# Scale-table quotients moved beside the attention outputs, and the maxima over partitions moved to TensorE, in a transformer layer kernel

## The reference

```python
x = hidden_states                       # (2, 1024, 1024) f32
xn = layernorm(x)
def bitnet_linear(x, weight, scale):    # q, k, v, o
    s = maximum(mean(abs(weight), axis=1), 1e-8)
    y = einsum('bsi,oi->bso', x, sign(weight / s[:, None])) * (s * scale)
    return nan_to_num(y, nan=0.0, posinf=1e6, neginf=-1e6)
# attention: 32 query heads, 8 key/value heads, head size 32, softmax(q k^T / sqrt(32)) v, then o
# feed forward: gate_w, up_w (1024, 3584), down_w (3584, 1024), int 0..15,
# zero point and scale for each group of 128 rows
def dequantize(w, scales, zeros):
    return (w - repeat(zeros, 128, axis=0)) * repeat(scales, 128, axis=0)
ffn = (silu(xn @ gate) * (xn @ up)) @ down
out = x + attention(xn) + ffn
```

## Time and profile before

| | |
|---|---|
| median of 3 runs | 2414.04 us (2412.61 to 2415.01) |
| the profiled execution's own time | 2414.68 us |
| its span, first to last instruction | 2412.7 us |
| PE busy | 2345.1 us (97%) |
| DVE busy | 1812.9 us (75%) |
| ACT busy | 1586.6 us (66%) |
| POOL busy | 963.6 us (40%) |
| mean granted TensorE clock | 0.994 |
| chain that ended last, by engine | PE 91%, DVE 4%, ACT 3%, issue 2% |

### The profile page before, as it was taken

How to read it: one execution, slowest core, us unless ns; L and a number is a source line. 1 busy time by engine, 2 the same in 40 slices (tenths; PEclk the granted TensorE clock), 3 DMA queues, 4 the chain that set the end, 5 groups by cost and what they waited for, 6 DMA issues and landing times.

```text
span 2412.7 us, 32718 instructions
## 1 busy us (share of the span) xinstructions
PE 2345.1 (97%) x12408; PEld 954.4 (40%) x12408; DVE 1812.9 (75%) x2313; ACT 1586.6 (66%) x2050; POOL 963.6 (40%) x533
## 2 busy tenths in 40 slices
PE   6999999999999999988999999999999999999998
PEld 3444233333333333323444444444444444444444
DVE  7878777777777777776467777777777777777777
ACT  5774777777777777774256666666665666666664
POOL 0000689999999999973012222220001222222000
PEclk9999999999999999999999999999999999999999
DMA  5220455555565555544311111131113211115111
GB/s 180 73 62 1 96 84 90 82 90 84 82 88 87 88 85 87 88 68 114 111 48 35 35 48 40 35 114 35 35 61 123 70 35 36 35 35 191 37 35 70
DMA packets 179857, 174.73 MB, mean 72 GB/s; under 512 B 87586, under 2 KB 127394, under 8 KB 179702
## 3 DMA queue, kind: packets, MB, share of 16 engines
q1 hardware_dynamic: 117430, 150.62, 20.3%
q0 software_dynamic: 62272, 22.03, 11.6%
HBM read 160.08 MB, written 65.45 MB: 93 GB/s over the span
## 4 chain that ended last, share of the span: by engine, by line
PE 91%; DVE 4%; ACT 3%; issue 2%; DMA 0%; SPq 0%; DVEq 0%; ACTq 0%; POOLq 0%
PE ps L1559 32%; PE ps L1575 16%; PE ps L1416 10%; PE ps L1361 10%; PE ps L1405 9%; PE ps L1429 5%; PE ps L1529 4%; PE ps L1381 3%; ACT zone L708 1%; DVE zone L973 0%; ACT zone L756 0%; ACT zone L822 0%; PE ps L1591 0%; DVE zone L1064 0%; ACT xT L678 0%
## 5 line engine op out<-in xcount | busy, mean ns | idle before, releaser
L1559 PE MATMUL ps<-xT,zone 128*128 128x512 f16 x3584 | 774.6, 379 | 2.7 <-DVE zone L1304 2.7
L1086 DVE TENSOR_REDUCE zone<-ps 128x1 f32<-128x512 f32 x1024 | 639.4, 683 | 178.7 <-PE ps L1361 178.6
L822 ACT ACTIVATE zone<-ps,sm 128x512 f32<-128x512 f32 x1024 | 626.8, 691 | 193.5 <-PE ps L1405 180.5
L599 POOL TENSOR_TENSOR zone<-zone 128x1024 f32<-128x1024 f32 x252 | 621.4, 2568 | 183.7 <-ACT zone L822 103.1
L1281 DVE TENSOR_SCALAR ps<-ps,zone_c 128x1024 f32<-128x1024 f32 x392 | 506.7, 1293 | 160.7 <-PE ps L1559 158.6
L889 ACT ACTIVATE ps<-ps,zone_c 128x1024 f32<-128x1024 f32 x392 | 426.7, 1088 | 259.9 <-PE ps L1559 259.9
L1559 PEld LDWEIGHTS ps<-xT,zone 128*128 128x128 f16 x3584 | 350.3, 98 | 426.2 <-DVE zone L1304 4.2
L1405 PE MATMUL ps<-zone 98*128 98x512 f16 x1024 | 388.3, 382 | 18.7 <-ACT zone L822 17.6
L1361 PE MATMUL ps<-zone 96*128 96x512 f16 x1024 | 388.3, 383 | 0.5 <-DVE zone L1086 0.4
L1575 PE MATMUL ps<-zone 128*128 128x512 f16 x1792 | 387.1, 379 | 0.0
L1292 DVE TENSOR_SCALAR ps<-ps,zone_c 128x1024 f32<-128x1024 f32 x216 | 279.3, 1293 | 93.0 <-PE ps L1575 92.8
(11 more groups left out here) (134 smaller groups left out, 1267.1 us busy)
## 6 DMA issues: line engine op xcount, KB each, us to landing
zone<-dequantised SPq DMA_DIRECT2D x84, 512.0 KB, 3.7
dequantised<-zero_points SPq DMA_DIRECT2D x84, 256.0 KB, 4.1
zone<-zone SPq DMA_DIRECT2D x384, 32.0 KB, 2.3
zone<-_attn_hidden_states_dram SPq DMA_DIRECT2D x16, 512.0 KB, 7.6
zone<-inverse_sums SPq DMA_DIRECT2D x128, 64.0 KB, 2.1
attention<-zone SPq DMA_DIRECT2D x32, 256.0 KB, 2.0
xT<-attention SPq DMA_DIRECT2D x4, 2048.0 KB, 11.9
dequantised<-in_L_ffn_gate_w_dram POOLq DMA_DIRECT2D x28, 256.0 KB, 6.2
```

Of the source, the lines that this page charges most:

```text
L599: nc.gpsimd.tensor_tensor(duo[n % 3], prob[:, prob_slot(e), :], prob[:, prob_slot(e + 2), :], add).then_inc(s["sum_ok"], 1)
L822: A(prob[:, prob_slot(e), m % 2 * 512:(m % 2 + 1) * 512], ps[:, 3 + m % 3, :], ACT.Exp, scale=gam[:, 0:1]).then_inc(s["exp_ok"], 1)
L1086: V.tensor_reduce(mxs[:, u % 2, half, i % 16:i % 16 + 1], ps[:, (2 * i + half) % 3, :], AX, amax).then_inc(s["max_ok"], 1)
L1559: last = MM(ps[:, 4 * s2 + 2 * m + c, :], ring[:, buf, m * H + g * P:m * H + (g + 1) * P], xT[:, hf, part, g, c * 512:(c + 1) * 512], star ...
```

## The change

- VectorE's `table_quotients` is cut into eight parts, `quotients(0)` to `quotients(7)`, which run behind the guards of outputs 13, 15, ... 27. `tab_ok` comes at the end of part 7. Nothing waits for it any more but ScalarE, after the last output.
- The maxima over partitions leave GpSimd. TensorE transposes the 128x56 maxima (`turn_maxima`, unit 30, behind step 11), VectorE reduces them along the row and scales a diagonal with them (`common_maxima`, its step 10), TensorE multiplies the diagonal with ones in four matmuls (`spread_maxima`, behind step 14), and VectorE multiplies the two halves (`common_product`, its step 11). Output 1 waits for that, as it uses the same PSUM bank.
- `load_wo(1)` follows `load_wo(0)` at step 15 of unit 30.
- The third round of `pair_sums` of unit 31 goes between the matmuls of output 0, the fourth behind output 1. ScalarE evacuates the sums behind output 1 and makes `head_of(30)` behind output 0; SP's three DMAs of the last inverse sums move from before output 0, 1 and 2 to 1, 2 and 4; VectorE's `invert(31)` moves from behind output 1 to behind output 2.

```diff
# SP
-                if u == UNITS - 1 and k == 3:
-                    sp.wait_ge(s["tab_ok"], 1)
                     load_wo(1)
...
-            compact_sums(UNITS - 1)
             for n in range(OUTPUTS):
                 if n == 1:
+                    compact_sums(UNITS - 1)
+                elif n == 2:
                     store_inverse(UNITS - 1)
-                elif n == 2:
+                elif n == 4:
                     spread_inverse(UNITS - 1)
# GpSimd
-            def common_maxima():
-                pool.wait_ge(s["pmx_ok"], 1)
-                nc.gpsimd.partition_all_reduce(pmr, pmx, P, RMAX).then_inc(s["pmr_ok"], 1)
-                pool.wait_ge(s["pmx_ok"], 2)
-                nc.gpsimd.partition_all_reduce(pmr2, pmx2, P, RMAX).then_inc(s["pmr_ok"], 1)
...
-                    if u == UNITS - 2 and j == 3:
-                        common_maxima()
# ScalarE, behind evac_attention(n)
                 if n == 0:
+                    head_of(UNITS - 2)
+                elif n == 1:
                     evacuate_sums(UNITS - 1)
-                    head_of(UNITS - 2)
# VectorE
-                ch.inc(V.tensor_reduce(cmx, tab, AX, amax, apply_absolute_value=True))
-                settle()
-                V.tensor_copy(pmx, cmx[:, :, 0]).then_inc(s["pmx_ok"], 1)
-                V.tensor_copy(pmx2, cmx[:, :, 1]).then_inc(s["pmx_ok"], 1)
+                V.tensor_reduce(cmx, tab, AX, amax, apply_absolute_value=True).then_inc(s["cmx_ok"], 1)
+                dve.wait_ge(s["cmx_ok"], 1)
+            def common_maxima():
+                dve.wait_ge(s["cmt_pe"], 1)
+                ch.inc(V.tensor_reduce(cmt, ps[0:2 * IT, 0, 0:P], AX, amax))
+                settle()
+                V.tensor_scalar(diag, id32[0:2 * IT, 0:2 * IT], cmt, None, mult).then_inc(s["dg_ok"], 1)
+            def common_product():
+                dve.wait_ge(s["pmr_pe"], 1)
+                both = ps[:, 1, 0:2 * IT].rearrange("p (t m) -> p t m", m=2)
+                ch.inc(V.tensor_copy(pmr2, both[:, :, 1]))
+                settle()
+                V.tensor_tensor(pmr, both[:, :, 0], pmr2, mult).then_inc(s["pmr_ok"], 1)
+                dve.wait_ge(s["pmr_ok"], 1)
+            def quotients(part):
+                if part == 0:
+                    dve.wait_ge(s["wosgn_ok"], 6)
+                    dve.wait_ge(s["woabs_ok"], 6)
+                    ...                       # floor and kept of tab, limited(tab)
+                elif part == 1:
+                    ...                       # reciprocal of tab
+                elif part == 2:
+                    ...                       # the two products of tab, first scale of pmr
+                elif part == 3:
+                    ...                       # reciprocal of pmr, its products with tab and dtab
+                elif part == 4:
+                    ...                       # maxima, floor and kept of dtab
+                elif part == 5:
+                    ...                       # limited(dtab)
+                elif part == 6:
+                    ...                       # reciprocal of dtab
+                elif part == 7:
+                    ...                       # the two products of dtab
+                    dve.sem_inc(s["tab_ok"], 1)
...
+                if u == UNITS - 2 and k == 10:
+                    common_maxima()
                 if k == 10 and u:
                     invert(u - 1)
                 if u == UNITS - 2 and k == 11:
-                    table_quotients()
+                    common_product()
...
                     output_magnitude(3)
-                    invert(UNITS - 1)
                 elif n == 2:
                     output_magnitude(4)
                     output_scales(1)
+                    invert(UNITS - 1)
...
+                elif 13 <= n < 28 and n % 2 == 1:
+                    quotients((n - 13) // 2)
# TensorE
+            def turn_maxima():
+                pe.wait_ge(s["cmx_ok"], 1)
+                TR(ps[0:2 * IT, 0, 0:P], cmx.rearrange("p t m -> p (t m)"), id32[:]).then_inc(s["cmt_pe"], 1)
+            def spread_maxima():
+                pe.wait_ge(s["dg_ok"], 1)
+                for h in range(4):
+                    last = MM(ps[32 * h:32 * h + 32, 1, 0:2 * IT], ones[0:2 * IT, :], diag, start=True, stop=True)
+                last.then_inc(s["pmr_pe"], 1)
...
-                if i == 0:
-                    pe.wait_ge(s["tab_ok"], 1)
...
+                if u == UNITS - 2 and k == 11:
+                    turn_maxima()
+                if u == UNITS - 2 and k == 14:
+                    spread_maxima()
...
+                if n == 1:
+                    pe.wait_ge(s["pmr_ok"], 1)
...
                 for kt in range(KT):
+                    if (n, kt) == (0, 4):
+                        pair_sums(UNITS - 1, 2)
...
-                if n == 0:
-                    pair_sums(UNITS - 1, 2)
+                if n == 1:
                     pair_sums(UNITS - 1, 3)
```

More of the change, by code:

```diff
@@ L247, in layer_kernel @@
         cm, cmr, fac, gam = cols(140, 3), cols(143, 3), cols(146, 3), cols(149, 1)
-        pmx, pmx2, pmr = (cols(190 + 28 * j, 28) for j in range(3))
-        pmr2 = cols(60, 28)
+        pmx, pmr, pmr2 = (cols(190 + 28 * j, 28) for j in range(3))
         inv = view(zone_b, 12, 448).rearrange("p (t m g) -> p t m g", t=IT, m=2)
@@ new lines, in _ @@
+            flat = tab.rearrange("p t m g -> p (t m) g")
+            floor, kept, few2 = flo[:, 0:56], own[:, 0:56], few.rearrange("p (a g) -> p a g", g=KT)
+            dmx, dfl, dkept = cmx.rearrange("p t m -> p (t m)")[:, 0:FQ], flo[:, 56:64], own[:, 56:64]
+            def quotients(part):
+                if part == 0:
+                    dve.wait_ge(s["wosgn_ok"], 6)
+                    dve.wait_ge(s["woabs_ok"], 6)
+                    most = cmx.rearrange("p t m -> p (t m)")
+                    ch.inc(V.tensor_scalar(floor, most, FLOOR, 1e-36, mult, amax))
+                    ch.inc(V.tensor_scalar(kept, most, 0.0, None, ALU.not_equal))
+                    settle()
+                    limited(flat, inv.rearrange("p t m g -> p (t m) g"), floor.unsqueeze(2).broadcast_to([P, 56, KT]), few2)
+                elif part == 1:
+                    ch.inc(V.reciprocal(inv, tab))
+                    settle()
+                elif part == 2:
+                    ch.inc(V.tensor_tensor(tab[:, :, :, 0:KT - 1], tab[:, :, :, 0:KT - 1], inv[:, :, :, 1:KT], mult))
+                    ch.inc(V.tensor_tensor(tab[:, :, :, KT - 1], tab[:, :, :, KT - 1], kept.rearrange("p (t m) -> p t m", m=2), mult))
+                    ch.inc(V.tensor_scalar(pmr, pmr, XS * XS, 1e-30, mult, amax))
+                    settle()
+                elif part == 3:
+                    ch.inc(V.reciprocal(pmx, pmr))
+                    settle()
+                    ch.inc(V.scalar_tensor_tensor(tab[:, :, 1, KT - 1], pmx, 2.0 ** -12, tab[:, :, 1, KT - 1], mult, mult))
+                    ch.inc(V.tensor_scalar(pmr, pmr, 2.0 ** 12, None, mult))
+                    settle()
+                    ch.inc(V.tensor_tensor(dtab, dtab, pmr.unsqueeze(2).broadcast_to([P, IT, FQ]), mult))
+                    settle()
+                elif part == 4:
+                    by_tile = dtab.rearrange("p t o -> p o t")
+                    ch.inc(V.tensor_reduce(dmx, by_tile, AX, amax, apply_absolute_value=True))
+                    settle()
+                    ch.inc(V.tensor_scalar(dfl, dmx, FLOOR, 1e-36, mult, amax))
+                    ch.inc(V.tensor_scalar(dkept, dmx, 0.0, None, ALU.not_equal))
+                    settle()
+                elif part == 5:
+                    limited(dtab, dinv, dfl.unsqueeze(1).broadcast_to([P, IT, FQ]), few[:, 0:224].rearrange("p (t o) -> p t o", t=IT))
+                elif part == 6:
+                    ch.inc(V.reciprocal(dinv, dtab))
+                    settle()
+                elif part == 7:
+                    ch.inc(V.tensor_tensor(dtab[:, 0:IT - 1, :], dtab[:, 0:IT - 1, :], dinv[:, 1:IT, :], mult))
+                    ch.inc(V.tensor_tensor(dtab[:, IT - 1, :], dtab[:, IT - 1, :], dkept, mult))
+                    settle()
+                    dve.sem_inc(s["tab_ok"], 1)
```

40 lines of the change are left out of this document (3 added, 37 removed).

## The result

The changed kernel takes 2401.67 us (median of 5 runs, 2399.55 to 2403.34), the kernel before 2413.41 (5 runs, 2412.31 to 2415.01). The ratio is 0.9952 with a 95% interval of 0.9941 to 0.9962: 11.7 us faster. The profiled execution of the changed kernel took 2399.88 us, its span is 2397.8.

A forecast was written before the change was run, and what follows sets the result against it. The prediction took TensorE's pause at step 8 of the last attention unit as the time to win: 13.0 + 1.5 + 0.45 - 0.5 - 0.35 = 14.1 us gained, so 2400.0 us, range 2397.5 to 2406.5.

The forecast's parts named there:

- What bounds the kernel: TensorE is busy 97% of the span; its longest single pause, 11.1 us, is in the last attention unit, step 8.
- two gates: At that pause exponentials wait for pair sums of both GpSimd and VectorE, ready within about a us of each other.
- Rival (b): One gate keeps closed, for instance GpSimd idles for another reason; pause of 7 to 9 us stays, 2411 us; chance 0.06.
- Part 1: Last attention unit: the pause and the half clock behind it go; gain 13.0 us.
- Rival (a): The pause in unit 31 only shrinks, as VectorE and GpSimd sums meet; gain 8 us, 2406 us; chance 0.16.
- Part 2: End of the denominators, first outputs: gain 1.5 us at VectorE's last pair sum and 0.45 ahead of output 6.
- Part 3: Work added on TensorE, one transpose and four matmuls; cost 0.5 us, between 0 and 1.5.
- Part 4: Last inverse sums, made later beside the outputs: ScalarE waits in `head_of(31)`, output 8 is late; cost 0.35 us, between 0 and 3.
- Part 5: VectorE's quotients beside outputs 13 to 27 fit into its idle time ahead of the guards; cost 0.
- Rival (c): Slower: the quotients become VectorE's bound at outputs 13 to 27; 2428 us; chance 0.03.

The follow-up runs named there:

- e1: The first experiment: the changed kernel with two idle reductions on GpSimd at the old place in unit 30; 2416.28 us in one run.
- the second experiment: The changed kernel with all eight parts of the quotients back in unit 30, the maxima staying on TensorE; 2413.94 us in one run.
- e7: The second experiment's kernel with two idle reductions on GpSimd added; 2415.7 us in one run.

## Why the prediction was right or wrong

The forecast was faster by 14.1 us, 2400.0 us; measured are 11.7 us and 2401.67, inside the range of 2397.5 to 2406.5. By the traces the change is worth 13.0 us. The 1.3 us between 13.0 and 11.7 lie within the scatter of the first stretch, and the interval of the ratio, 9.2 to 14.2 us, holds both. Step by step:

- **What bounds the kernel.** Right: one pause with two gates. The first and the second experiment each closed one gate again, and got 10.8 and 12.4 us of pause. The 12.4 are more than VectorE's own work: GpSimd, no longer away, held VectorE up by some 7 us (a block of 24.8 us, 17.9 in e7). (The rest of TensorE's list of waits is not all of the first stage, as the prediction has it: some 4.8 us of it lie in the feed forward, which took 1189.2 us in both kernels.) Rival (b), that GpSimd idles for another reason than the reductions, is refuted: in the changed kernel its idle times of 6.4 and 7.1 us are gone, and with idle reductions they are back. The rule that I had weighed against it (the Trainium skill, GPSIMD Engine Reference, 4.1 Engine selection) gives reductions along the partitions to GpSimd; following it was the dearer choice here: the rows have 1 us of work in 14 us of GpSimd's time, and the way over TensorE cost 0.23 us on the path.
- **Part 1, 13.0 us.** Measured 23.16 - 9.92 = 13.24. What is late next is the alternation of ScalarE and TensorE, as said: waits of 0.19 to 0.62 us. The signs of the output weight were rightly charged to this stretch. Rival (a), that the pause only shrinks, did not come about; VectorE's sum took 2.06 us in the overlap and was still early.
- **Part 2, 1.5 and 0.45 us.** Output 3 begins 1.47 us earlier counted from output 0, and the wait ahead of output 6 is gone. Both terms were right in themselves and brought nothing (part 4); had the product come at the median of the traces with this order, 25.74, the outputs would have lost 0.3 us on top (118.30 us in e1).
- **Part 3, -0.5 us.** From the tables to step 6 it is 19.96 us against 19.73 (1075.56 - 1055.60, 1077.24 - 1057.51): 0.23. The transpose and the four matmuls, 0.6 us together, lie partly in the waits for ScalarE, and neither they nor VectorE were late.
- **Part 4, -0.35 us.** This is the term that was mis-sized. The mechanism was the one described: ScalarE waits in `head_of(31)` behind output 4, and output 8 is late through VectorE's guards. The size was 1.9 us: output 8 begins 33.72 us behind output 0 in both kernels, so the 1.47 and 0.45 of part 2 are all given back. I had the copy of `head_of(31)` begin at 24.6 us; it began at 26.7 (1117.36 - 1090.66). The step that failed is "from the issue of the spread to the product of GpSimd it was 3.37 us": it became 5.0, since the change lets a load of 512 KB and a store of 256 KB go ahead of the spread. The issue itself came at 20.4 (1111.06), 0.4 later than reckoned. That the load is all of it is not shown: where it was moved away, the small store landed late instead, and the product came at 25.0 all the same. From the product on each us counts fully: in all seven traces with `head_of(31)` behind output 4 and the new order of the pair sums, output 8 begins 8.31 to 8.33 us behind the product (25.40 and 33.72 in the changed kernel, 24.95 and 33.27 with the load behind the spread, 26.23 and 34.55 at the latest). The bounds, 0 and 3, held it. Two of the signs that the prediction named were missed here: 5.44 us in `head_of(31)` where it said some 3, and 1.11 us ahead of output 8 where it said under 1.
- **Part 5, 0 us.** Right. The parts took 2.4, 3.0 and 0.8 us where the largest were put at 2.5, 3.0 and 1.5, and leaving them out gains nothing. Rival (c), that they bind at outputs 13 to 27, is refuted by the 83 us without a pause of TensorE.
- **The range.** The scatter of the first stretch, some 4 us between single runs, was no term of the sum; three runs of before, within 2.4 us, did not show it.

## What to carry to other kernels

When a pause has several gates that open almost together, price the change by what is late once all of them are gone, and check each gate by closing it alone. When a DMA of a chain is moved to a later place in its queue, cost it with what now goes ahead of it there, not with its old landing time, and read several traces of one order before believing a difference of half a us. And put the instruction that waits for such a chain as late on its engine as its own consumer allows: that move was worth 1.9 to 2.1 us here, all that the outputs had given back.

## What the runs showed of the hardware

- **A reduction over partitions on GpSimd cost 14 us of its time for 1 us of work.** In three profiles with two `partition_all_reduce` in a row, GpSimd stood idle 6.2 to 6.7 us ahead of them and 6.7 to 7.3 us behind, with nothing in the profile to wait for. The same maxima by a transpose, a reduction of 56x128, a product with a diagonal and four matmuls took 0.30, 0.28, 0.33 and 0.30 us.
- **A small VectorE instruction can stand still for several GpSimd instructions that follow each other without a gap.** A product of 56 columns in SBUF took 10.13 us beside a subtraction, three sums and a division of GpSimd, 6.43 beside a subtraction and two sums, and 0.12 when GpSimd was idle. Other VectorE instructions were not held: the reciprocal of 448 columns took 2.95 us beside a subtraction and a sum of GpSimd before the change, and 2.96 with GpSimd idle. The Trainium skill (GPSIMD Engine Reference, 8. Key points) names contention for the SBUF interfaces with VectorE instructions in a 2-port mode or with two SBUF inputs. The rows agree that there is one; they show besides that an instruction may have to wait for several of GpSimd's, not for one. The product has a single SBUF tensor input; no trace shows in which mode it ran.
- **A DMA of 8 KB landed after 1.4 to 3.7 us** (`store_inverse(31)`, eleven traces), and after 1.6 to 3.7 in seven traces with one and the same order of DMAs on SP.
- **A load of 512 KB right ahead of four DMAs of 64 KB held up their consumer**: 4.5 to 5.4 us from the issue of the spread to GpSimd's product in seven traces with the load issued up to 2.6 us ahead, 3.3 to 3.5 in three traces without it and in one with it 2.8 us ahead.
